# A cross-attention, self-attention and expert block: self-attention four slots later, batches normalised in two slots

## The chip, the core and the metric

One core of a Trainium2 chip. Its engines are TensorE (PE in the rows; PEld is its loading of weights), VectorE (DVE), ScalarE (ACT), GpSimd (POOL) and SyncE (SP), which issues most of the DMAs. Each runs its own list of instructions in order; semaphores tie the lists together. The metric is device time in microseconds; lower is better.

## What is computed

Eight batches of 64 latent rows of 512 attend to a context of 1601 rows, then to themselves, and then go through experts:

```python
def stablemax(x):
    s = jnp.where(x >= 0, x + 1.0, 1.0 / (1.0 - x))
    return s / jnp.sum(s, axis=-1, keepdims=True)
...
x = x + xattn(layernorm(x), ctx_1024, ...)   # 16 heads of 32, q, k, v, stablemax(q k / sqrt(32)) v, Wo
x = x + attn(layernorm(x), ...)              # 8 query heads of 64, one k and v, causal softmax, Wp
x = x + ffn(layernorm(x), ...)               # mean of 2 shared experts + top 2 of 8 routed, gelu, 512 -> 2048 -> 512
```

x is (8, 64, 512), ctx_1024 is (8, 1601, 512), all in float32.

## The kernel before

**Slots.** The first part is a list of 104 slots (`NCH`), 13 for each of 8 batches, one for each piece of 128 context rows and one for the tail of 65. I call a batch's slots r0 to r12; slot n is r(n mod 13) of batch n // 13. Every engine walks the same slots, `for n in range(NSLOT)`, with its own order of calls in a slot. Slots 104 to 135 hold the shared experts, and the routed experts come after them.

**Keys and values.** Context comes in 24 parts, three for a batch (r0 to r3, r4 to r7, r8 to r12). A part's keys and values are made from seven block products each (`product`, L928 and L931), Strassen's way. VectorE makes sums of the context (`context_sum`, L1572), ScalarE casts a block (`context_hi`, L1330), GpSimd subtracts the cast from it (`context_lo`, L685), TensorE multiplies, and VectorE joins the product into keys or values (`joined`, L1591 to L1611). In a part's first slot stand VectorE's three context sums for the next part, in its second the casts and subtractions of six blocks, in its third those of block 6. The key product for which a block is needed stands in the slots after.

**Scores and weights.** `scores` (L951) fills a bank for two pieces, in even slots of a batch; it waits until all earlier weights are made. ScalarE makes Relu, Ln and Exp of them (L1442, L1451, L1455), VectorE the weights (`weights`, L1623), TensorE the weighted values (`weighted`, L970), and GpSimd adds the weights up (`sums`, L731, in the slot after). The tail's scores are r12. After a batch, `denominators` (L981) and `normalised` (L1747 to L1761, five instructions for each half of the batch) finish it, three and four slots later.

**Self-attention.** Three of its four tiles (two batches each) run beside later batches. Their steps have fixed distances d from the first, `slot_of(t, d)`: the output projection and its stats (d=0, L996), the rows (d=1, L743 on GpSimd), their transposes (2, L1028), queries (3, L1037), keys and values (4), scores and masking (5), exponentials (5 and 6, on ScalarE), softmax and scaling (7, L1676 and L748), transposes (8), the attended values (9, L1077, then L1695 and L1697 on VectorE), the projection (11, L1091), the rows again (12), transposes (13) and gates (14). Before, tile t begins in slot 32 + 26 t, which is r6. `halved` says in which slots ScalarE casts the two output weights (L1368); GpSimd subtracts them one slot later (`output_weights_lo`, L758, the long one).

**Banks.** Products, and most steps of the self-attention, take one of three PSUM banks in turn (`pj`, `take`): each waits until VectorE has read what stood in its bank three uses ago.

**Experts.** A unit is a quarter of an expert's weights, 128x2048. It lands in a ring of eight; ScalarE casts it (`weights_hi`, L1378), VectorE subtracts (`weights_split`, L1721), and each copy has three places. `shared_up` (L1146), `gelu`, `hidden` (L1730, L1732) and `shared_down` (L1166) follow one another, two steps to a unit. The order in which VectorE takes the work of a slot is written out by hand:

```python
if n == NCH - 4:
    weights_split(0)
...
for p_ in products(n)[:before]:
    joined(*p_)
for m in group(n - 1)[1:] + group(n)[:1]:
    weights(m, 0)
    weights(m, 1)
for p_ in products(n)[before:]:
    joined(*p_)
...
for b, g, m in finished(n)[1]:
    normalised(b, g, m)
```

## Time and profile before

| | us |
|---|---|
| median of 3 runs (lowest, highest) | 1241.25 (1239.51, 1242.89) |
| the profiled execution | 1241.11 |
| its span, first to last instruction | 1239.4 |
| TensorE busy | 1210.2 (98%) |
| VectorE busy | 839.8 (68%) |
| ScalarE busy | 687.0 (55%) |
| GpSimd busy | 571.7 (46%) |

The busy shares are means over the whole span. In the stretch from 100 to 700 us GpSimd is busy some 70% and VectorE 74% of the time; in the stretch of the experts GpSimd hardly works. Idle time of an engine other than TensorE costs something only where TensorE waits for it, so the stops of TensorE are to be read one by one, with what the other engines did before each.

### The profile page before, as it was taken

The numbers are of one execution on the slowest core, as the hardware profiler recorded it, in microseconds if no ns is written. First come the engines' busy times: TensorE is split into PE (matmuls) and PEld (weight loads), VectorE is DVE, ScalarE is ACT, GpSimd is POOL, SyncE is SP. The second block draws the span as 40 slices with busy tenths as digits, with TensorE's granted clock in tenths as the row PEclk, the third lists the DMA queues.
The fourth block names the chain that finished last, engine by engine and source line by source line (L and its number), as shares of the span: only waits on it lengthen the run. The fifth ranks groups of instructions, "written<-read, shape, count | busy, mean of one in ns | idle before, by whom it ended". The sixth has DMA issues, their size and how long they took to land.

```text
span 1239.4 us, 33792 instructions
## 1 busy us (share of the span) xinstructions
PE 1210.2 (98%) x14478; PEld 1133.6 (91%) x14478; DVE 839.8 (68%) x1265; ACT 687.0 (55%) x1236; POOL 571.7 (46%) x357
## 2 busy tenths in 40 slices
PE   8999999999999999999999998999999999999998
PEld 7899999989999989999989997898889999999997
DVE  7666786776777686786785875766676455555655
ACT  4366656745755655756656557555644445544443
POOL 5656767776758776867766764000041001000000
PEclk9999999999999999999999998899999999999999
DMA  7331111121121212012112123745455599999991
GB/s 268 121 105 40 41 40 37 44 73 67 41 82 39 76 70 70 23 67 74 41 70 74 36 107 146 306 172 179 170 191 208 192 362 345 346 338 354 355 384 36
DMA packets 34794, 179.40 MB, mean 145 GB/s; under 512 B 6264, under 2 KB 9496, under 8 KB 15568
## 3 DMA queue, kind: packets, MB, share of 16 engines
q1 hardware_dynamic: 32896, 172.42, 38.0%
q0 software_dynamic: 1744, 4.76, 1.2%
q8 instruction: 117, 1.92, 0.6%
q14 instruction: 37, 0.30, 0.1%
HBM read 168.97 MB, written 8.19 MB: 143 GB/s over the span
## 4 chain that ended last, share of the span: by engine, by line
PE 91%; DVE 4%; issue 2%; POOL 1%; ACT 1%; DMA 0%; DVEq 0%; SPq 0%; POOLq 0%
PE bank L928 18%; PE bank L931 18%; PE bank L1285 12%; PE sc L1302 9%; PE sc L951 7%; PE sc L1146 7%; PE bank L970 4%; PE sc L1166 4%; PE bank L1166 4%; PE bank L909 1%; PE bank L1037 1%; DVE tt L1623 1%; POOL xn L731 1%; PE bank L1091 1%; PE bank L996 1%
## 5 line engine op out<-in xcount | busy, mean ns | idle before, releaser
L731 POOL TENSOR_TENSOR xn<-xn,tt 128x1024 f32<-128x1024 f32 x96 | 231.9, 2416 | 165.1 <-DVE tt L1623 163.3
L931 PE MATMUL bank<-wvh,blk 128*128 128x256 f32 x1344 | 248.8, 287 | 5.3 <-DVE va L1594 5.3
L928 PE MATMUL bank<-blk,wkh 128*128 128x256 f32 x1344 | 246.0, 285 | 0.0
L1721 DVE TENSOR_TENSOR wsl<-ring,wsh 128x2048 fp32r<-128x2048 f32 x72 | 165.2, 2294 | 112.6 <-ACT wsh L1378 109.8
L1442 ACT ACTIVATE tt<-sc 128x512 f32<-128x512 f32 (+1 forms) x208 | 107.8, 603 | 217.1 <-PE sc L951 209.3
L931 PEld LDWEIGHTS bank<-wvh,blk 128*128 128x128 f32 x1344 | 209.9, 192 | 8.8 <-DVE va L1594 6.1
L928 PEld LDWEIGHTS bank<-blk,wkh 128*128 128x128 f32 x1344 | 209.2, 192 | 4.2 <-issue 1.6
L931 PE MATMUL bank<-wvl,blk 128*128 128x256 f32 x672 | 190.6, 284 | 0.0
L928 PE MATMUL bank<-blk,wkl 128*128 128x256 f32 x672 | 190.0, 283 | 0.0
L1378 ACT CAST wsh<-ring 128x2048 fp32r<-128x2048 f32 x72 | 137.4, 1909 | 45.8 <-PE sc L1302 21.2
L1285 PEld LDWEIGHTS bank<-xT,ring 128*128 128x128 f32 x1280 | 144.8, 192 | 1.0
L1285 PE MATMUL bank<-xT,ring 128*128 128x128 f32 x1280 | 144.8, 275 | 0.0
L1623 DVE SCALAR_TENSOR_TENSOR tt<-sc,tt 128x512 f32<-128x512 f32 (+1 forms) x208 | 132.9, 680 | 0.8 <-ACT tt L1455 0.8
L931 PEld LDWEIGHTS bank<-wvl,blk 128*128 128x128 f32 x672 | 129.4, 193 | 0.0
L928 PEld LDWEIGHTS bank<-blk,wkl 128*128 128x128 f32 x672 | 128.8, 192 | 0.0
L685 POOL TENSOR_TENSOR blk<-bsum,blk 128x512 fp32r<-128x512 f32 x96 | 124.1, 1321 | 6.1 <-DVE bsum L1572 4.8
L1451 ACT ACTIVATE tt<-tt 128x512 f32<-128x512 f32 (+1 forms) x208 | 121.2, 644 | 0.0
L1455 ACT ACTIVATE tt<-tt 128x512 f32<-128x512 f32 (+1 forms) x208 | 120.9, 643 | 0.0
L951 PEld LDWEIGHTS sc<-qc,kk 32*128 32x128 f32 x3072 | 91.7, 189 | 11.9 <-DVE tt L1623 4.3
L951 PE MATMUL sc<-qc,kk 32*128 32x64 f32 x3072 | 98.3, 276 | 4.1 <-DVE tt L1623 4.1
L685 POOL TENSOR_TENSOR blk<-stg,blk 128x512 fp32r<-128x512 f32 x72 | 97.1, 1362 | 1.8 <-ACT blk L1330 1.8
L843 POOL DMA_INDIRECT yrows<-xT,tabi x7 | 6.9, 988 | 193.2 <-ACT xT L1518 193.2
(327 smaller groups left out, 2204.9 us busy)
## 6 DMA issues: line engine op xcount, KB each, us to landing
ring<-in_w SPq DMA_DIRECT2D x112, 1024.0 KB, 6.1
stg<-in_ctx SPq DMA_DIRECT2D x24, 1024.0 KB, 5.0
wqt<-in_wo SPq DMA_DIRECT2D x4, 1024.0 KB, 5.0
wqt<-in_aq SPq DMA_DIRECT2D x4, 1024.0 KB, 5.0
wqt<-in_ap_ SPq DMA_DIRECT2D x4, 1024.0 KB, 4.9
yrows<-K SPq DMA_DIRECT2D x1, 2048.0 KB, 12.4
bsum<-in_tails SPq DMA_DIRECT2D x2, 520.0 KB, 6.6
ktail<-bsum SPq DMA_DIRECT2D x1, 1040.0 KB, 4.1
```

The costliest lines, as they stand in the source:

```text
L685: e.tensor_tensor(block_lo(i, j), block_raw(i, j), block_hi(i, j).bitcast(F32), ALU.subtract).then_inc(s["cl_pool"], 1)
L731: e.tensor_tensor(dacc[0:kn, y, :], dacc[0:kn, y, :], tt[0:kn, w, :], ALU.add).then_inc(s["da_pool"], 1)
L928: m = e.matmul(dst[:, 256 * a:256 * a + 256], w[:, WPOS[j], c, r], x[:, c, :], start=(k_ == 0), stop=(k_ == 5))
L931: m = e.matmul(dst[:, 256 * a:256 * a + 256], x[:, c, r], w[:, WPOS[j], c, :], start=(k_ == 0), stop=(k_ == 5))
L951: m = e.matmul(sc[0:kn, h, c0 + 64 * g:c0 + 64 * g + 64], key, qc[r, g, 64 * b:64 * b + 64], start=True, stop=True)
L1285: m = e.matmul(bank[q % 2][:, P * jj:P * jj + P], ring[slot(un)][:, 512 * c + P * jj:512 * c + P * jj + P], xg[:, y, c, :], start=(c == 0) ...
L1302: m = e.matmul(bank[2][:], h_[:, j, :], w_[r_ % 3][:, 512 * jj:512 * jj + 512], start=(j == 0 and x_ == 0), stop=(j == 15 and x_ == 2))
L1378: e.copy(wsh[m % 3][:], ring[slot(un)][:]).then_inc(s["wh_act"], 1)
L1451: e.activation(tt[0:kn, w, r], tt[0:kn, w, r], ACT.Ln, bias=1.0).then_inc(s["ln_act"], 1)
L1455: e.activation(tt[0:kn, w, r], tt[0:kn, w, r], ACT.Exp, scale=-1.0).then_inc(s["ex_act"], 1)
L1623: e.scalar_tensor_tensor(t_, score_read(n, kn, hb), 0.0, t_, ALU.max, ALU.add).then_inc(s["f_dve"], 1)
L1721: e.tensor_tensor(wsl[m % 3][:], ring[slot(unit_split(m))][:], wsh[m % 3][:].bitcast(F32), ALU.subtract).then_inc(s["wl_dve"], 1)
```

## The change

The self-attention of tiles 0 to 2 begins four slots later (slot 36 + 26 t, which is r10), and so do its loads of weights. Only the gates of tile 2 stay in slot 104. The casts of the output weights move to three slots ahead of the first step and to d=6 (slots 33 and 42 for tile 0, where they were 27 and 37). A batch is normalised half in r3 and half in r5. ScalarE's cast of block 6 in r10 stands behind the exponentials, where it stood between Relu and Ln. At the end of the 104 slots VectorE splits unit 0 behind its weights of slot 100; unit 2 is copied and subtracted by VectorE alone (`weights_second`, in slots 100 and 102, the copy in place of ScalarE's in slot 104); the weights of piece 101 are made in slot 102. TensorE makes `shared_up(1)` in slot 102 and `shared_up(2)` in slot 104, where it made them in slots 103 and 106. The ring of three banks begins with bank 7, and the first tail value products wait accordingly. In the diff a line of semaphore names is cut; `first_dve` is added to it.

```diff
--- before.py
+++ after.py
@@ -107,8 +107,8 @@
             den.append(b)
             if last:
                 nrm.append((b, 0, 4))
-        if lag == 4 and not last:
-            nrm += [(b, 0, 2), (b, 2, 2)]
+        if lag in (4, 6) and not last:
+            nrm.append((b, lag - 4, 2))
     return den, nrm
 
 
@@ -120,7 +120,7 @@
 
 def halved(slot, what):
 
-    return next((t for t in range(3) if slot == (slot_of(t, 0) - 5, slot_of(t, 5))[what]), None)
+    return next((t for t in range(3) if slot == (slot_of(t, 0) - 3, slot_of(t, 6))[what]), None)
 
 
 def slot_of(t, d):
@@ -129,7 +129,7 @@
         return NCH + 2 + LAST_TILE[d]
     if t == 2 and d == 14:
         return NCH
-    return 2 * PER * t + 2 * PER + 6 + (9 if d == 10 else d)
+    return 2 * PER * t + 2 * PER + 10 + (9 if d == 10 else d)
 
 
 def tile(slot, d):
@@ -363,13 +363,13 @@
...
-        bank_read = [st.enter_context(nc.semaphore(f"bank{i}_read")) for i in (0, 1, 7)]
+        bank_read = [st.enter_context(nc.semaphore(f"bank{i}_read")) for i in (7, 0, 1)]
@@ -378,7 +378,7 @@
         ring_in = [st.enter_context(nc.semaphore(f"ring{i}_in")) for i in range(NR)]
         b1_in = [st.enter_context(nc.semaphore(f"b1_{k}_in")) for k in range(NBLK)]
 
-        pj = [bank[0], bank[1], bank[7]]
+        pj = [bank[7], bank[0], bank[1]]
         uses = projections()
         use = {u: n for n, u in enumerate(uses)}
         pob = bank[6]
@@ -418,6 +418,13 @@
         def unit_split(m):
 
             return m if m < 32 else unit_routed(*divmod(m - 32, 4), 1)
+
+        def wait_split(e, m):
+
+            if m == 2:
+                e.wait_ge(s["first_dve"], 2)
+            else:
+                e.wait_ge(s["wl_dve"], m + (m < 2))
 
         def slot(n):
             return n % NR
@@ -584,14 +591,14 @@
 
                 m = n - NR
                 if m < 32:
-                    e.wait_ge(s["wl_dve"], m + 1)
+                    wait_split(e, m)
                 else:
                     k, r = divmod(m - 32, 8)
                     kind, q = divmod(r, 4)
                     if kind == 0:
                         e.wait_ge(s["ru_pe"], 4 * k + q + 1)
                     else:
-                        e.wait_ge(s["wl_dve"], 32 + 4 * k + q + 1)
+                        wait_split(e, 32 + 4 * k + q)
 
             e.wait_ge(s["s_pe"], NCH - 1)
             load_shared(5)
@@ -899,7 +906,7 @@
                 dst, kn = take("vt", j), (8 if j == 4 else P)
                 col = 260 * (j // 2) + P * (j % 2)
                 if j < 3:
-                    e.wait_ge(s["kt_dve"], (10, 12, 8)[j])
+                    e.wait_ge(s["kt_dve"], (8, 10, 12)[j])
                 if j == 4:
                     e.wait_ge(s["tl_dve"], 3)
                 for c in range(4):
@@ -1127,7 +1134,7 @@
                 p, r = divmod(s_, NSH)
                 un = unit_shared(s_, 0)
                 if s_ % 2 == 0:
-                    e.wait_ge(s["wl_dve"], un + 1)
+                    wait_split(e, un)
                 if s_ < 2:
                     take("up", s_)
                 elif s_ < 4:
@@ -1152,13 +1159,13 @@
                 p, r = divmod(s_, NSH)
                 un = unit_shared(s_, 1)
                 if s_ % 2 == 0:
-                    e.wait_ge(s["wl_dve"], un + 1)
+                    wait_split(e, un)
                 e.wait_ge(s["hd_dve"], 2 * s_ + 2)
                 if s_ == 0:
                     e.wait_ge(s["f_dve"], 2 * NCH)
                 elif s_ == NSH:
                     e.wait_ge(s["un_dve"], NB)
-                    e.wait_ge(bank_read[2], reads_up_to(last_use(2)))
+                    e.wait_ge(bank_read[0], reads_up_to(last_use(0)))
                 for i in range(2):
                     for t in range(2):
                         c0 = 256 * i + P * t
@@ -1171,7 +1178,7 @@
             def positions():
 
                 e.wait_ge(s["rt_dve"], RT_SEL8)
-                for b_ in range(2):
+                for b_ in range(1, 3):
                     e.wait_ge(bank_read[b_], reads_up_to(last_use(b_)))
                 for t in range(4):
                     for t_ in range(t + 1):
@@ -1226,11 +1233,9 @@
                 if tile(n, 9) is not None:
                     for b in range(2):
                         attended(tile(n, 9), b)
-                if n == NCH - 1:
-                    shared_up(1)
                 for m in group_before(n):
                     weighted(m)
-                if NCH + 1 < n < NCH + 2 * NSH:
+                if NCH + 2 < n < NCH + 2 * NSH:
                     shared_up(n - NCH)
                 if tile(n, 2) is not None:
                     turn_rows(tile(n, 2))
@@ -1242,6 +1247,9 @@
                     product(*made_)
                 if n == NCH - 2:
                     shared_up(0)
+                    shared_up(1)
+                if n == NCH:
+                    shared_up(2)
                 if n == PLACE:
                     positions()
                 if n == PLACE + 2:
@@ -1295,7 +1303,7 @@
                 for q in range(4):
                     r_ = 32 + 4 * k + q
                     e.wait_ge(s["rh_dve"], 2 * (4 * k + q) + 2)
-                    e.wait_ge(s["wl_dve"], r_ + 1)
+                    wait_split(e, r_)
                     for jj in range(4):
                         j = 4 * q + jj
                         for x_, (h_, w_) in enumerate(((hTh, wsh), (hTh, wsl), (hTl, wsh))):
@@ -1441,8 +1449,6 @@
                     for hb in range(2):
                         e.activation(weights_view(m, kn, hb), score_read(m, kn, hb), ACT.Relu,
                                      scale=-1.0).then_inc(s["t_act"], 1)
-                if d == 2 and last and i + 1 < NPART:
-                    context_hi(i + 1, 6)
                 for m in group(n):
                     w, kn = m % TR, tokens(m)
                     for hb in range(2):
@@ -1453,6 +1459,8 @@
                         r = slice(512 * hb, 512 * hb + 512)
                         e.wait_ge(s["ln_act"], 2 * m + hb + 1)
                         e.activation(tt[0:kn, w, r], tt[0:kn, w, r], ACT.Exp, scale=-1.0).then_inc(s["ex_act"], 1)
+                if d == 2 and last and i + 1 < NPART:
+                    context_hi(i + 1, 6)
                 if d == 1 and i + 1 < NPART:
                     for j in ORDER[:6]:
                         context_hi(i + 1, j)
@@ -1474,9 +1482,7 @@
                     weights_hi(1)
                 if NCH <= n < NCH + 2 * NSH:
                     gelu(n - NCH)
-                    if n == NCH:
-                        weights_hi(2)
-                    elif n - NCH + 2 < 32:
+                    if NCH < n < NCH + 30:
                         weights_hi(n - NCH + 2)
                 if tile(n, 5) == 3:
                     for half in range(2):
@@ -1717,9 +1723,21 @@
                 e.tensor_tensor(gates[:, t, :], pj_of("g", t)[:, 0:8], rbt[:], ALU.add).then_inc(read_of("g", t), 1)
 
             def weights_split(m):
-                e.wait_ge(s["wh_act"], m + 1)
+                e.wait_ge(s["wh_act"], m + (m < 2))
                 e.tensor_tensor(wsl[m % 3][:], ring[slot(unit_split(m))][:], wsh[m % 3][:].bitcast(F32),
                                 ALU.subtract).then_inc(s["wl_dve"], 1)
+
+            def weights_second(lo):
+
+                if lo:
+                    e.wait_ge(s["v_pe"], PROD * NPART)
+                    e.wait_ge(s["first_dve"], 1)
+                    m = e.tensor_tensor(wsl[2][:], ring[slot(2)][:], wsh[2][:].bitcast(F32), ALU.subtract)
+                else:
+                    e.wait_ge(ring_in[slot(2)], ring_value(2))
+                    e.wait_ge(s["v_pe"], PROD * NPART - 5)
+                    m = e.tensor_copy(wsh[2][:], ring[slot(2)][:])
+                m.then_inc(s["first_dve"], 1)
 
             def hidden(s_):
                 e.wait_ge(s["ge_act"], s_ + 1)
@@ -1926,8 +1944,6 @@
                 last = i % PER_BATCH == PER_BATCH - 1
                 if n % PER == 0 and 0 < n <= NCH:
                     batch_sums(n // PER - 1)
-                if n == NCH - 4:
-                    weights_split(0)
                 if n == NCH - 1:
                     weights_split(1)
                 if d == 0 and i + 1 < NPART:
@@ -1976,18 +1992,24 @@
                 before = ((2, 1, 2, 1, 1) if last else (2, 0, 2, 0))[d]
                 for p_ in products(n)[:before]:
                     joined(*p_)
+                if n == NCH - 2:
+                    weights_second(1)
+                    weights(n - 1, 0)
+                    weights(n - 1, 1)
                 for m in group(n - 1)[1:] + group(n)[:1]:
-                    weights(m, 0)
-                    weights(m, 1)
+                    if m != NCH - 3:
+                        weights(m, 0)
+                        weights(m, 1)
                 for p_ in products(n)[before:]:
                     joined(*p_)
                     if p_ == ("v", i, 4) and i + 1 < NPART:
                         context_sum(i + 1, 3)
+                if n == NCH - 4:
+                    weights_split(0)
+                    weights_second(0)
                 for b, g, m in finished(n)[1]:
                     normalised(b, g, m)
 
-                if n == NCH + 1:
-                    weights_split(2)
                 if NCH <= n < NCH + 2 * NSH:
                     hidden(n - NCH)
                     if n > NCH and n - NCH + 2 < 32:
```

## Rows read from the trace of the kernel before

**Rows 1.** The page, busy time, share of the span and instructions of each engine.

```profile
PE 1210.2 (98%) x14478; PEld 1133.6 (91%) x14478; DVE 839.8 (68%) x1265; ACT 687.0 (55%) x1236; POOL 571.7 (46%) x357
```

**Rows 2.** TensorE's own waits: line, releaser, us in total, times, longest us.

```profile
PE sc L951 <- DVE tt L1623: 10.2, 8, 4.1
PE bank L931 <- DVE va L1594: 5.3, 3, 1.8
PE bank L909 <- issue: 2.6, 1, 2.6
...
PE bank L981 <- POOL xn L731: 1.3, 1, 1.3
...
PE sc L1166 <- issue: 0.8, 1, 0.8
```

**Rows 3.** Windows: us, each engine's busy us (instructions), TensorE's clock, DMA share, GB/s.

```profile
262.30:265.60 3.30, 3.30 (x17) 3.30 (x17) 3.20 (x7) 1.02 (x2) 1.93 (x1) 0.50 0.03 7
...
753.80:760.60 6.80, 5.32 (x128) 5.20 (x128) 2.03 (x4) 1.48 (x4) 2.36 (x1) 0.50 0.09 17
```

**Rows 4.** A window with L928 alone: us, TensorE matmul and weight load, clock, DMA.

```profile
242.00:253.00 11.00, 10.34 (x84) 10.13 (x84) 1.00 0.32 110
```

**Rows 5.** A window with L996 alone, the same columns.

```profile
268.00:273.00 5.00, 2.97 (x12) 2.19 (x12) 1.00 0.05 8
```

**Rows 6.** Timeline of VectorE, slot 29: start us, us, engine, line, operation, tiles, count.

```profile
253.08 0.94 DVE L1747 RECIPROCAL xT<-xT 128x128 f32<-128x128 f32 x1
254.06 2.00 DVE L1751 TENSOR_TENSOR xT<-xT 128x128 f32<-128x128 f32 x1
...
258.78 0.29 DVE L1761 TENSOR_TENSOR cTl<-xT,cTh 128x128 fp32r<-128x128 f32 x1
```

**Rows 7.** Timeline of TensorE: scores of r8, r10, tail (bare batch), tail (attention beside it).

```profile
196.99 2.01 PE L951 MATMUL sc<-qc,kk 32*128 32x64 f32 x64
...
208.78 2.01 PE L951 MATMUL sc<-qc,kk 32*128 32x64 f32 x64
...
219.74 0.70 PE L951 MATMUL sc<-qc,ktb 32*65 32x64 f32 x32 [0.54 <-DVE tt L1623]
...
315.32 0.70 PE L951 MATMUL sc<-qc,ktb 32*65 32x64 f32 x32 [1.32 <-DVE tt L1623]
```

**Rows 8.** Timeline of ScalarE, r10 of the bare batch.

```profile
210.94 2.07 ACT L1442 ACTIVATE tt<-sc 128x512 f32<-128x512 f32 x4 [0.98 <-PE sc L951]
213.54 0.62 ACT L1330 CAST blk<-stg 128x512 fp32r<-128x512 f32 x1 [0.53 <-PE bank L931]
...
217.20 1.13 ACT L1455 ACTIVATE tt<-tt 128x512 f32<-128x512 f32 x2
```

**Rows 9.** Timeline of GpSimd: two sums, a block subtraction, the weights' subtraction, a scaling.

```profile
193.73 4.91 POOL L731 TENSOR_TENSOR xn<-xn,tt 128x1024 f32<-128x1024 f32 x2
...
217.77 1.31 POOL L685 TENSOR_TENSOR blk<-stg,blk 128x512 fp32r<-128x512 f32 x1
...
246.43 4.63 POOL L758 TENSOR_TENSOR wol<-wqt,woh 128x2048 fp32r<-128x2048 f32 x1
...
326.68 1.05 POOL L748 TENSOR_TENSOR sm<-sm,rs 128x512 f32<-128x512 f32 x1 [4.37 <-DVE rs L1676]
```

**Rows 10.** Timeline of VectorE: a context sum and a cast beside GpSimd, a sum alone.

```profile
43.86 1.77 DVE L1572 TENSOR_TENSOR bsum<-stg 128x512 f32<-128x512 f32 x1
...
46.46 1.23 DVE L1826 CAST blank<-xa 128x15 f32<-128x15 int32 x1
...
198.78 0.69 DVE L1572 TENSOR_TENSOR bsum<-stg 128x512 f32<-128x512 f32 x1 [1.00 <-DMA stg<-in_ctx]
```

**Rows 11.** Timeline of VectorE, slot 100.

```profile
750.97 2.46 DVE L1721 TENSOR_TENSOR wsl<-ring,wsh 128x2048 fp32r<-128x2048 f32 x1 [1.57 <-ACT wsh L1378]
```

**Rows 12.** Timeline of GpSimd and VectorE, slot 44.

```profile
362.47 2.08 POOL L743 TENSOR_SCALAR xa<-xres,mv,rstd 128x512 f32<-128x512 f32 x1
...
363.20 0.68 DVE L1572 TENSOR_TENSOR bsum<-stg,bsum 128x512 f32<-128x512 f32 x1
```

More of the change, by code:

```diff
@@ L365, in build @@
             "exp_act woh_act xh_act gap_act wT_act ge_act wh_act rg_act yh_act "
-            "eps_dve iota_dve ones_dve cs_dve un_dve wkl_dve wvl_dve tl_dve kt_dve bias_dve xr_dve f_dve "
+            "eps_dve iota_dve ones_dve cs_dve un_dve first_dve wkl_dve wvl_dve tl_dve kt_dve bias_dve xr_dve f_dve "
             "cr_dve bn_dve xn_dve xa_dve xt_dve sm_dve oh_dve nrm_dve xl_dve rt_dve hd_dve "
```

## The prediction

> **What bounds the kernel now.** I read the page first: TensorE is busy 98% of the span [rows 1], so the end moves only if its stops, its clock or its work change. The change leaves TensorE's work as it is. The list of TensorE's own waits comes next [rows 2]: 10.2 us before the scores (L951), 5.3 us before value products (L931), 2.6 us at the start (L909), 1.3 and 0.8 us at the hand-over to the experts. With smaller ones that is about 24 us in a span of 1239.4; from 777 us to 1231 us there is no stop over 0.1 us, so all that can be won or lost lies in the first 777 us, and a microsecond of stop there is a microsecond of the end. Third, the granted clock: after some stops it falls from 2.4 to 1.2 GHz for 3.4 or 6.8 us [rows 3]; every microsecond of work in such a stretch loses half a microsecond. It did so after the stop before L909 and after the 4.1 us stop, after one of three stops of 1.75 us and one of five of 1.3 us.
>
> I write r0 to r12 for the slots of a batch. A product lasts 1.48 us (7 in 10.34) [rows 4], the output projection 2.9 us [rows 5].
>
> **What it saves.**
> (a) Batches normalised in two slots. Vector's ten instructions of the batch before, at the end of r3, last 6.0 us (253.08 to 259.07) in the slots 29, 55 and 81, since the first tensor_tensor takes 2.00 us instead of 0.29 while GpSimd runs [rows 6]; the copy of value product 0 comes late and product 3 waits for its bank: 5.3 us in 3 stops [rows 2]. Half the work, 2.1 us, now goes to r5, and GpSimd's 4.63 us subtraction [rows 9] no longer stands in r2, so the first half is free of it too. The copy ends before it is wanted: -5.3 us, and the half clock after the first of these stops [rows 3] goes with it, -1.7 us.
> (b) The stop before the tail's scores (r12) is 1.32 us with the self-attention's masking beside it and 0.54 us in a bare batch [rows 7]. All become bare: 3 x 0.78, -2.3 us. The 0.54 stays: it is the joining of a key product and then the weights, on Vector, not ScalarE's cast, which is also moved.
> (c) The end. Vector's split of unit 0 (2.46 us, after 1.57 us of waiting for ScalarE) stands ahead of the weights for which the scores wait 4.1 us [rows 11, 2]. Placed behind them, the stop becomes the 0.6 us of (b). Unit 2 split early lets its first product fill the stretch before the denominators. But shared_up(1) no longer covers ScalarE's and Vector's 4.8 us from the tail's scores to its weights: 2.6 us of small matmuls are left, so 2.2 to 2.4 us of stop. Then 1 us each before the down product 0 and the output of tile 3 and about 1 us before the down product 2 (Vector's halving waits for the table loads after the root). Stops and half clock of before there are 6.4 and 5.6 us; what I get for after is 7.0 us. I take -5 us; bounds -8 and 0.
> (d) Ring turned: the first tail value product waits for kt_dve 8, not 10, and starts when TensorE is free, but the transposes behind still wait for kt_dve 16. Between 0 and -1.4 us: -0.7.
> Together -15.0 us.
>
> **What it costs.**
> (e) Rows for the self-attention, now r10 to r12. TensorE reaches r10 at S (208.78 in a bare batch, [rows 7]), spends 2.9 us on the output, and starts its scores at S+2.9. ScalarE begins 2.16 us later; Relu, Ln and Exp of both tiles last 6.2 us without the cast between them [rows 8], to S+11.3. The cast of block 6 (0.62 us), which stood between Relu and Ln, now comes only here: S+11.8. GpSimd, in its own order, must then subtract block 6 (1.31 us) [rows 9], add a sum (2.4 us), and only then make the rows (a TENSOR_SCALAR, 2.08 us) [rows 12]: S+17.6. TensorE has done tail scores and two weighted tiles at S+15.5 (219.74 - 208.78 + 2.9 + 1.66) and stands at the transposes, three key products queued behind: 2.1 us of stop, three times, +6.3. Lower bound 0.5 us each if the cast's place didn't matter, upper 3.
> (f) Second half of the normalising, r5, before the attention's output in r6. Vector's instruction with two SBUF inputs, or a CAST, ends only when GpSimd's running tensor_tensor ends: the last of three sums beside GpSimd took 1.77 us instead of 0.69, a 15-element CAST 1.23 us [rows 10]. In r5 GpSimd runs its six block subtractions without a pause, 1.3 us each, and it is late there: scaling (1.05 us) waits for Vector and holds up a sum, then the 4.63 us subtraction [rows 9]. With P the start of r4's scores, GpSimd starts the train at P+15.7; Vector starts its half at P+15.4, passes the reciprocal (0.94 us, not held: [rows 6]) and then pays one GpSimd instruction for each of four: done at P+21.0 instead of P+17.5, and two of its four copies of the attended rows (0.43 us each) free the first bank at P+21.9. TensorE wants it for the second key product at P+18.7. That is 3.2 us for tiles 0 and 1, and 0.8 us for tile 2, whose batch has two instructions fewer: +7.2, bounds 2 and 11.
> (g) GpSimd's other 4.63 us subtraction moves from r2 to r8. It starts when two sums end (198.64) [rows 9], and Vector's first context sum is issued at 198.78 [rows 10]. The sum is held to 203.3, the third ends at 205.1, value product 0 is joined at 205.8; TensorE wants its bank at 204.4 (scores at 196.99 [rows 7], plus 3.0, plus three products). 1.4 us in three batches: +4.2, bounds 0 and 6.
> (h) In the four batches without attention in r6 the half of (f) delays the joining of key product 0, which the fourth needs. Vector frees it at about P+21.9, TensorE wants it at P+20.7; one GpSimd boundary earlier there is no stop. Half of 4 x 1.2: +2.4, bounds 0 and 5.
> (i) Clock. Two stops over 3 us, three of 2.1 and one of 2.4: by the shares above some three falls, 1.7 us each, less what the followers catch up: +4, bounds 0 and 9.
> Moved at no cost: ScalarE's two casts of output weights (1.9 us, in r3 and r7, where it idles 7 us), the three loads of weights on SyncE (each has two slots to land in; the context loads behind them wait for GpSimd anyway; in the last batch they now follow the experts' first three loads, by which they are not delayed), the joins, which keep their order.
>
> A row where a page and the trace part: Vector's sum beside GpSimd's TENSOR_SCALAR (L743) took 0.68 us, not held at all [rows 12]. The Trainium skill (SBUF — State Buffer, two separate sides) says that the shared port pair is an exclusive lock for the whole instruction, against any GpSimd instruction that reads SBUF. By the page the split of unit 0 in slot 100, which meets L743, would wait about 1 us more and the end would gain 4 us rather than 5; by the row it doesn't, and the sum above goes by the row.
>
> **Sum.** -15.0 + 6.3 + 7.2 + 4.2 + 2.4 + 4 = +9.1 us on the profiled execution's 1241.11 (span 1239.4 and 1.7 around it): 1250.2. The median shown is 1241.25, so I say 1250.
>
> **Rivals.**
> (1) The holding of Vector doesn't reach TensorE (it decides at P+18.7: if Vector has freed the attended bank by then, and the context sums of r8 slip in before GpSimd's long subtraction). Then (f), (g), (h) are nothing and (i) about 2: 1241.1 - 15 + 6.3 + 2 = 1234.4; with (g) alone left, 1239. For it: GpSimd and Vector meet only within tenths. Against: GpSimd has no idle time in r5 in any batch. Faster, 0.25, mostly 1233 to 1237.
> (2) Savings and costs cancel: two of (e) to (h) at their lower bounds, or one halved and the clock never falling: 1238 to 1244. 0.17.
> (3) The hand-over is worse: up(0) waits for the bank of the third transposes, which Vector reads only behind two 2.3 us instructions, and the saving of (c) is 0; with the clock falling often: 1256 to 1262. 0.10.
> (4) All stops go as the placing suggests and no new ones come: 1241.1 - 19 (with the 4.1 us stop's full 9 us): 1222 to 1230. 0.05.
> The forecast itself, 1245 to 1256, has 0.43. Range 1233 to 1258.
>
> About 0.3% (3.7 us) can be told from no change. Faster by more: rival 1 without its upper tail and rival 4, 0.26. Within: rival 2 and that tail, 0.21. Slower: the forecast and rival 3, 0.53.
>
> **What would show it.** Gone: the stops before L931 in r4, the 1.32 us ones, the 4.1 us one. New, in the list of TensorE's waits: three of about 2 us before the transposes of self-attention rows (L1028 of before) put down to GpSimd's rows; two of 3 us before a key product (L928), released by Vector's L1697; three of 1.4 us before L931 in r8. In Vector's rows: the tensor_tensors of the second half at 1.2 us instead of 0.29, and a context sum of over 4 us in r8. It is wrong if those rows are short, or if GpSimd has its rows ready when TensorE comes.

## The result, and the profile after

| | before | after |
|---|---|---|
| median, us (lowest, highest) | 1241.08 (1239.51, 1242.89) | 1253.95 (1253.73, 1256.09) |
| ratio, with its 95% interval | | 1.0108 (1.0092 to 1.0124) |
| the profiled execution, us | 1241.11 | 1256.09 |
| its span, us | 1239.4 | 1254.3 |

The changed kernel is 1.1% slower; 1250 was forecast. The profiled execution of after is the slowest of its four, so what follows explains 14.9 us of span, of which the medians show 12.9.

First TensorE's own waits after the change (line, releaser, us in total, times, longest us). Lines have moved by some seven: L935 and L938 are the key and value products, L958 the scores, L977 the weighted values, L1014 transposes at the start, L1035 the transposes of self-attention rows, L1173 the experts' down product.

```profile
PE bank L1035 <- POOL xa L750: 6.2, 3, 2.1
PE bank L935 <- DVE oTl L1703: 5.9, 2, 2.9
PE sc L958 <- DVE tt L1629: 5.0, 9, 0.6
PE bank L935 <- DVE kk L1597: 4.6, 4, 1.1
PE sc L1014 <- DVE bsum L1554: 2.8, 1, 2.8
PE bank L977 <- DVE tt L1629: 2.2, 1, 2.2
PE bank L938 <- DVE va L1600: 2.0, 3, 0.8
...
PE sc L1173 <- DVE hl L1750: 1.4, 1, 1.4
```

Beside [rows 2] the reader sees what left: of 10.2 us before the scores 5.0 remain, the three stops before the value product in r4 are gone, and those of the hand-over shrank from 6.4 to 5.4 us, the scores' there included. What came is larger: the first, second, fourth and seventh row, 18.7 us. All stops together (over 0.1 us, without the 1.1 us ahead of TensorE's first instruction) are 34.9 us; they were 23.8.

The granted clock, in the windows in which it fell after such a stop (columns as in [rows 3]):

```profile
312.30:315.70 3.40, 3.40 (x19) 3.40 (x17) 1.21 (x2) 0.00 (x0) 1.79 (x1) 0.51 0.02 5
373.80:377.20 3.40, 3.40 (x19) 3.40 (x18) 2.50 (x6) 0.00 (x0) 3.40 (x3) 0.50 0.00 0
561.50:564.90 3.40, 3.40 (x18) 3.40 (x17) 2.49 (x6) 0.00 (x0) 3.40 (x3) 0.50 0.02 5
786.80:793.60 6.80, 6.58 (x60) 6.22 (x64) 3.89 (x5) 5.72 (x7) 4.63 (x3) 0.50 0.35 113
```

The first follows one of the three 2.1 us stops, the second and third the two of 2.9 us, the last the 2.2 us stop of the hand-over. Each 3.4 us at 1.2 GHz, with TensorE busy throughout, costs 1.7 us.

Where the second kind of stop comes from stands in the timelines of slot 43 (r4) to 45 (r6), first VectorE's (start us, us, engine, line, operation, tiles, shapes, count, idle before it and its releaser):

```profile
366.72 0.94 DVE L1765 RECIPROCAL xT<-xT 128x128 f32<-128x128 f32 x1
367.70 0.72 DVE L1769 TENSOR_TENSOR xT<-xT 128x128 f32<-128x128 f32 x1
368.46 1.27 DVE L1775 TENSOR_TENSOR xT<-xT,bvt 128x128 f32<-128x128 f32 x1
369.76 1.19 DVE L1777 CAST cTh<-xT 128x128 fp32r<-128x128 f32 x1
370.98 1.26 DVE L1779 TENSOR_TENSOR cTl<-xT,cTh 128x128 fp32r<-128x128 f32 x1
372.17 0.41 DVE L1701 CAST oTh<-bank 128x256 fp32r<-128x256 f32 x1
372.61 0.42 DVE L1703 TENSOR_TENSOR oTl<-bank,oTh 128x256 fp32r<-128x256 f32 x1
```

then GpSimd's and TensorE's in the same stretch:

```profile
366.99 2.59 POOL L692 TENSOR_TENSOR blk<-stg,blk 128x512 fp32r<-128x512 f32 x2
369.53 5.09 POOL L692 TENSOR_TENSOR blk<-bsum,blk 128x512 fp32r<-128x512 f32 x4
...
373.09 0.50 PE L935 MATMUL bank<-blk,wkh 128*128 128x256 f32 x2 [2.94 <-DVE oTl L1703]
```

Where nothing holds them the tensor_tensors last 0.29 us [rows 6] and the cast 0.23 us, as this row of the kernel before shows:

```profile
256.42 0.23 DVE L1759 CAST cTh<-xT 128x128 fp32r<-128x128 f32 x1
```

Here the four last 0.72, 1.27, 1.19 and 1.26 us: each ends with the block subtraction of GpSimd (1.3 us) beside it, the first having come in the middle of one. The two instructions behind them (L1701, L1703) read the PSUM bank and take 0.41 and 0.42 us in the midst of GpSimd's next subtractions, not held. The attended values wait behind the four, and TensorE waits for their bank. That is step (f), as forecast.

The context sum of r8 beside GpSimd's long subtraction, VectorE and then GpSimd:

```profile
282.94 4.87 DVE L1578 TENSOR_TENSOR bsum<-stg 128x512 f32<-128x512 f32 x1
287.85 0.69 DVE L1578 TENSOR_TENSOR bsum<-stg,bsum 128x512 f32<-128x512 f32 x1
...
282.66 4.61 POOL L765 TENSOR_TENSOR wol<-wqt,woh 128x2048 fp32r<-128x2048 f32 x1
```

The sum, alone 0.69 us [rows 10], ends 0.54 us after GpSimd does. Of this kind of holding the Trainium skill (SBUF — State Buffer, SBUF: two separate sides) says that whichever of the two starts first has the shared ports for its whole instruction, where VectorE's has two SBUF inputs or runs in a two-port mode. By that rule, the trace agrees for the rows above in how the wait ends (with an instruction of GpSimd, never shared out). The first sum's row names stg once since both of its inputs lie there.

### The profile page after: what moved, and what is told of

It is laid out like the page before. It is cut to its first block, busy times and chain, and to the rows that moved or that the text cites. A ratio compares the mean times of both kernels' runs of the same rounds, so it can differ in the third digit from the quotient of the medians.

```text
span 1254.3 us, 33794 instructions
## 1 busy us (share of the span) xinstructions
PE 1214.3 (97%) x14478; PEld 1135.4 (91%) x14478; DVE 873.1 (70%) x1266; ACT 685.0 (55%) x1235; POOL 574.0 (46%) x357
## 4 chain that ended last, share of the span: by engine, by line
PE 77%; DVE 10%; issue 6%; POOL 5%; DMA 1%; ACT 1%; SPq 0%; DVEq 0%; POOLq 0%; ACTq 0%
PE bank L938 14%; PE bank L935 14%; PE bank L1293 11%; PE sc L1310 9%; PE sc L1153 7%; PE sc L958 5%; PE bank L1173 4%; PE sc L1173 3%; PE bank L977 3%; POOL blk L692 2%; POOL xn L738 2%; DVE tt L1629 1%; DVE bsum L1578 1%; PE bank L1044 1%; PE bank L916 1%
## 5 line engine op out<-in xcount | busy, mean ns | idle before, releaser
L935 PE MATMUL bank<-blk,wkh 128*128 128x256 f32 x1344 | 251.0, 288 | 10.6 <-DVE oTl L1703 5.9
L938 PE MATMUL bank<-wvh,blk 128*128 128x256 f32 x1344 | 247.8, 286 | 2.1 <-DVE va L1600 2.0
L935 PEld LDWEIGHTS bank<-blk,wkh 128*128 128x128 f32 x1344 | 212.7, 195 | 16.4 <-DVE oTl L1703 6.3
L938 PEld LDWEIGHTS bank<-wvh,blk 128*128 128x128 f32 x1344 | 208.8, 191 | 5.9 <-DVE va L1600 2.7
L935 PE MATMUL bank<-blk,wkl 128*128 128x256 f32 x672 | 192.1, 286 | 0.0
L938 PE MATMUL bank<-wvl,blk 128*128 128x256 f32 x672 | 190.0, 283 | 0.0
L935 PEld LDWEIGHTS bank<-blk,wkl 128*128 128x128 f32 x672 | 130.9, 195 | 0.0
L938 PEld LDWEIGHTS bank<-wvl,blk 128*128 128x128 f32 x672 | 128.7, 192 | 0.0
L958 PEld LDWEIGHTS sc<-qc,kk 32*128 32x128 f32 x3072 | 90.1, 187 | 8.3 <-issue 2.2
L958 PE MATMUL sc<-qc,kk 32*128 32x64 f32 x3072 | 96.7, 273 | 0.5 <-DVE tt L1629 0.5
```

Source lines behind the costliest of these rows:

```text
L935: m = e.matmul(dst[:, 256 * a:256 * a + 256], w[:, WPOS[j], c, r], x[:, c, :], start=(k_ == 0), stop=(k_ == 5))
L938: m = e.matmul(dst[:, 256 * a:256 * a + 256], x[:, c, r], w[:, WPOS[j], c, :], start=(k_ == 0), stop=(k_ == 5))
L958: m = e.matmul(sc[0:kn, h, c0 + 64 * g:c0 + 64 * g + 64], key, qc[r, g, 64 * b:64 * b + 64], start=True, stop=True)
```

## The experiments

Two theories. **Mine:** VectorE's instructions on SBUF are held by whatever GpSimd runs beside them, and GpSimd's rows come late, so each new stop belongs to one named pair of instructions and goes with it. **The rival:** VectorE or GpSimd has simply too much work in these slots, and a stop that is removed comes back one slot later. Each run was timed beside the kernel before; ratios are to that.

### ScalarE's cast of block 6 where it was

```diff
+                if d == 2 and last and i + 1 < NPART:
+                    context_hi(i + 1, 6)
                 for m in group(n):
                     w, kn = m % TR, tokens(m)
...
-                if d == 2 and last and i + 1 < NPART:
-                    context_hi(i + 1, 6)
```

> The changed kernel with ScalarE's cast of block 6 in r10 back between Relu and Ln; nothing else. Theory (GpSimd's order behind a late cast): the three stops of 2.1 us before the self-attention's transposes shrink to about 0.5 us, since GpSimd has block 6 by S+9 and then waits only for the weights; 1254.0 becomes 1248 to 1250, with one clock fall fewer. Rival (GpSimd has simply too much work in r9 to r11, wherever the cast stands): the stops stay at 2 us and the time at 1254.

1246.35 us (1242.50 to 1250.26), ratio 1.0047 (1.0031 to 1.0062). TensorE's waits of this kernel:

```profile
PE bank L935 <- DVE oTl L1703: 5.9, 2, 3.0
...
PE bank L935 <- DVE kk L1597: 4.6, 4, 1.2
...
PE bank L1035 <- POOL xa L750: 1.6, 3, 0.5
```

The three stops of 2.1 us are now 0.5 us, and no other stop changed by more than 0.5 us but one of 1.0 us at the hand-over, which is new: the cast's place made 4.7 us of stops. The median fell by 7.6 us, more than that, since the clock falls less often: in the profiled run it fell once after the start, for 3.4 us.

### GpSimd's rows ahead of its sums

```diff
+                if tile(n, 1) is not None and tile(n, 1) < 3:
+                    rows(1, tile(n, 1))
                 if 1 <= n < NCH + 1:
                     sums(n - 1)
...
-                if tile(n, 1) is not None and tile(n, 1) < 3:
-                    rows(1, tile(n, 1))
```

> The changed kernel with GpSimd making the self-attention's rows ahead of the sum in the same slot (r11) instead of behind it. Theory: rows end at S+15.3 instead of S+17.6 and TensorE comes at S+15.5: the three stops of 2.1 us go, 1254.0 becomes 1246 to 1248. Rival (ScalarE's root or the stats are late, not GpSimd's order): the stops stay. Rival 2 (the postponed sum is wanted sooner): a new stop of up to 2 us elsewhere in r12 or r0.

1246.41 us (1244.14 to 1249.36), ratio 1.0045 (1.0030 to 1.0060). The wait for GpSimd's rows is gone from the list altogether (6.2 us), and no new one of over 0.3 us appeared. So the order in GpSimd's queue, cast then subtraction then sum then rows, is the whole of step (e). This run has less stop than the last (29.1 us for 29.9) and the same time: its clock fell three times after the start, for 17 us together.

### All of the batch normalised in r3 again

```diff
-        if lag in (4, 6) and not last:
-            nrm.append((b, lag - 4, 2))
+        if lag == 4 and not last:
+            nrm += [(b, 0, 2), (b, 2, 2)]
```

> The changed kernel with a batch normalised in one slot again (r3), self-attention still four slots later. Theory (the half in r5 is held up by GpSimd's block subtractions): both stops of 2.9 us in r6 and the four of 1.14 us go, with two clock falls; in r4 at most 0.2 us comes back, since GpSimd's long subtraction no longer makes its sums late in r3: 1239 to 1242. Rival (the stop in r6 comes from the two banks that the attended rows take, whatever Vector did before): the 2.9 us stay, and the three 1.75 us stops in r4 return: 1254 to 1260.

1252.93 us (1249.52 to 1253.80), ratio 1.0089 (1.0071 to 1.0106): the time was missed by 11 us. Its waits:

```profile
PE bank L1035 <- POOL xa L750: 6.3, 3, 2.1
...
PE bank L935 <- POOL blk L692: 4.1, 7, 0.7
...
PE bank L938 <- DVE va L1600: 2.8, 3, 1.3
```

Both stops for the attended values' bank and all four before the joining of the first key product went (10.5 us), so the half in r5 made steps (f) and (h). But two others grew behind them: GpSimd's block subtractions now come late before the key products of r6, and the value product in r8 waits 1.3 us instead of 0.8 in two of three batches, as TensorE arrives without the stop ahead (in the third 0.2 us, behind a new wait of 0.7 us before L977). Stops fell only from 34.9 to 31.1 us. The three 1.75 us stops of r4 did not come back although all ten instructions stand in r3 again: in the kernel before they were not the ten instructions' doing alone. My mechanism held, and the rival holds for over half of the gain.

### GpSimd's first long subtraction in r2 again

```diff
-    return next((t for t in range(3) if slot == (slot_of(t, 0) - 3, slot_of(t, 6))[what]), None)
+    return next((t for t in range(3) if slot == (slot_of(t, 0) - 9, slot_of(t, 6))[what]), None)
```

> The changed kernel with the first cast of output weights and GpSimd's 4.6 us subtraction in the slots where they were before (27 and 28 for tile 0, r1 and r2), not in r7 and r8. Theory (Vector's context sum in r8 is held by that subtraction): the stops of 0.5 to 0.8 us before L938 in r8 go, -2 us, 1252; the first half of the normalising is held by 1.7 us again but no stop follows from it. Rival (the r8 stops are a consequence of the later r5 half alone): they stay, 1254.

1260.45 us (1256.40 to 1261.04), ratio 1.0146 (1.0127 to 1.0164), slower than the changed kernel by 6.5 us where 2 us less were expected. The stops in r8 went, as my theory said, but one wait grew:

```profile
PE bank L935 <- DVE kk L1597: 7.9, 4, 2.3
```

It was 4.6 us; three of its four stops are now 2.2 us. In sum the stops are 36.0 us, 1.1 more than in the changed kernel. What made it slower is the clock: it fell nine times in the profiled run, five times in the changed kernel's. So this 4.6 us instruction costs stops in both slots in which it stood. That isn't so in every slot: behind the one for the second output weight, where the kernel before has it (here tile 0's), no stop came for 84 us.

```profile
317.69 4.62 POOL L758 TENSOR_TENSOR wol<-wqt,woh 128x2048 fp32r<-128x2048 f32 x1
```


### The end alone, on the kernel before

The kernel before with the hunks of the diff that touch the experts' first units and the weights of slots 101 and 102. The ring of banks stays as it was; the text below names it among the edits, but the run left it out.

```diff
+                if n == NCH - 2:
+                    weights_second(1)
+                    weights(n - 1, 0)
+                    weights(n - 1, 1)
...
+                if n == NCH - 4:
+                    weights_split(0)
+                    weights_second(0)
...
                     shared_up(0)
+                    shared_up(1)
+                if n == NCH:
+                    shared_up(2)
```

> The kernel before with the edits of the end alone (splits of units 0 to 2, order of the weights of slots 101 and 102, shared_up(1) and (2) earlier, ring of banks turned); self-attention, casts and normalising as before. Theory: the end's saving doesn't depend on the rest: the 4.1 us stop becomes about 0.6, a stop of about 2.3 us comes between shared_up(2) and the weighted values, three of about 1 us at the experts; 1241 less 2 to 5 us, 1236 to 1239, less if the half clock after 787 us stays as long as 6.8 us. Rival (the end's saving is given back in the experts whatever stands ahead): 1241, no change.

1236.49 us (1233.61 to 1238.26), ratio 0.9966 (0.9956 to 0.9976), on a kernel before of 1240.42: 3.9 us faster. The waits and the clock at the hand-over:

```profile
PE bank L977 <- DVE tt L1629: 2.2, 1, 2.2
...
PE sc L1173 <- DVE hl L1750: 1.4, 1, 1.4
```

```profile
770.23:773.64 3.41, 3.41 (x17) 3.20 (x16) 3.31 (x2) 3.39 (x5) 2.88 (x2) 0.50 0.24 41
```

Step (c) is right in mechanism and size: the 4.1 us stop is 0.5 us, and 2.2 us come behind `shared_up(2)`. The routed experts begin 4.3 us earlier relative to the first batch. In the changed kernel the same stop was followed by 6.8 us of half clock instead of 3.4, and 1.7 us of this gain were lost.

### Two slots of normalising alone, on the kernel before

The diff is the third experiment's, turned round.

> The kernel before with the batches normalised in two slots (r3 and r5) and nothing else. The self-attention of before begins in r6, so no attended values wait for a bank in r6; GpSimd's subtraction of the first output weight still stands in r2. Theory: the three stops of 1.75 us before the value product in r4 go (-5.3 us); the half in r5 meets GpSimd's train of block subtractions, is held, and the joining of the first key product of r6 comes 1 us late in each of the seven batches: +7 to +8 us of stops of 1.1 us. 1241 -5.3 +7.5 and one or two more half-clock stretches: 1243 to 1247. Rival (the holding is no cost without the attention beside it): 1241 -5.3 = 1236, and no stop over 0.5 us before the key products of r6.

1269.16 us (1268.01 to 1269.64), ratio 1.0230 (1.0213 to 1.0247). Both numbers given were far off. TensorE's waits and, below, VectorE in slot 31 (r5):

```profile
PE bank L996 <- issue: 26.4, 3, 8.8
```

```profile
268.24 0.94 DVE L1747 RECIPROCAL xT<-xT 128x128 f32<-128x128 f32 x1
...
271.36 1.17 DVE L1759 CAST cTh<-xT 128x128 fp32r<-128x128 f32 x1
272.56 2.33 DVE L1761 TENSOR_TENSOR cTl<-xT,cTh 128x128 fp32r<-128x128 f32 x1
```

I had overlooked who reads the second half: the self-attention's output projection, the first step of r6 in the kernel before. TensorE stands at it for 8.8 us in each of three batches; the clock fell 2.2 to 2.4 us into each of these stops and stayed low for 10.2 us, 3.6 to 3.8 of them with TensorE back at work; the last of the held instructions waits for a sum of GpSimd, 2.33 us. The stops of r4 did go. So the two edits belong together: normalising in two slots is possible only with the self-attention later.

### The self-attention four slots later alone, on the kernel before

```diff
-    return 2 * PER * t + 2 * PER + 6 + (9 if d == 10 else d)
+    return 2 * PER * t + 2 * PER + 10 + (9 if d == 10 else d)
...
-    return next((t for t in range(3) if slot == (slot_of(t, 0) - 5, slot_of(t, 5))[what]), None)
+    return next((t for t in range(3) if slot == (slot_of(t, 0) - 3, slot_of(t, 6))[what]), None)
```

> The kernel before with the self-attention (and its loads and casts) four slots later, and nothing else: all of a batch still normalised in r3, ScalarE's cast of block 6 where it was, the end as before. Theory: the three stops of 1.32 us before the tail's scores become 0.54 (-2.3 us); the rows of r11 come late by GpSimd's sum alone, 0.5 us (three times) since the cast is early; GpSimd's 4.63 us subtraction, now in r8, holds a context sum: three stops of 1.3 us before value products in r8 and, behind it, about 0.65 us twice a batch in r6 (three batches) as in the run with one slot of normalising. The 1.75 us stops of r4 are not there, because they came of the subtraction in r2. 1241 -2.3 -5.3 +1.5 +4 +4 = 1243, and up to three more half-clock stretches: 1243 to 1249. Rival (the 1.75 us stops come of the ten instructions standing in one slot, whatever GpSimd does): they stay, and the time is 1248 to 1254.

1248.16 us (1246.15 to 1250.49), ratio 1.0056 (1.0039 to 1.0073), inside what was expected, and the stops that were named are there (in r8 two of three at their size, the middle one 0.4 us):

```profile
PE sc L951 <- DVE tt L1623: 8.1, 8, 4.3
PE bank L928 <- POOL blk L685: 4.0, 6, 0.7
PE bank L931 <- DVE va L1594: 3.0, 3, 1.3
...
PE bank L1028 <- POOL xa L743: 1.6, 3, 0.5
```

The 1.75 us stops before L931 in r4 went with GpSimd's subtraction out of r2, with all ten instructions still in one slot; the rival is out for these. But the sum of stops doesn't give the time. They are 27.4 us against 23.8 before, the clock was low for as long (but before, 1.5 us of it lay in a stop and cost nothing), and the span is 9.4 us longer. The larger part is in no stop: from the tail of the second batch to that of the fourth TensorE took 177.2 us outside its stops and half clock before, and 179.2 us here, with as many instructions. Over the three tiles that is 5.2 us (2.0, 2.1 and 1.1). By pairs of neighbouring matmuls it lies in front of products and of L1077, in steps of 0.1 to 0.25 us, and behind each listed stop the next matmul starts some 0.15 to 0.27 us late. I call these small waits; which of them has which cause I can't tell from the trace. They don't come with the later self-attention alone. Counted in the same way against "the end alone" (the kernel before in the first two stretches), they are 3.0 us in the changed kernel, 5.3 us with all of a batch normalised in r3 again, and 0.9 us with the first long subtraction back in r2, though the self-attention is late in all three. So the place of that subtraction bears on them as well; how much stays open, since the last of these kernels also had 24 us of half clock in these stretches, where such waits could hide, and the changed one 10 us.

### The second half in r6

```diff
-        if lag in (4, 6) and not last:
-            nrm.append((b, lag - 4, 2))
+        if lag in (4, 7) and not last:
+            nrm.append((b, 2 * (lag > 4), 2))
```

> The changed kernel with the second half of the normalising one slot later, in r6, where GpSimd's train of block subtractions has ended. Theory: the held half was the cause of the two 2.9 us stops (attended values' bank) and of four 1.1 us ones before the key products of r6; with the half out of r5 they go: -10.5 us of stops and one clock stretch less, but the value products' stops in r8 grow from 0.7 to 1.3 us (three times, +1.5): 1254 -10.5 -1.7 +1.5 = 1243, range 1241 to 1247. Rival (Vector is late there for the amount of its work in r4 to r6, not for the holding): the stops move by a slot and the time stays at 1252 to 1256.

1263.77 us (1261.12 to 1265.76), ratio 1.0186 (1.0168 to 1.0204). My number was 20 us too low and even the rival's too low. The stops of steps (f) and (h) went and larger ones came: 9.2 us before the attended values' projection (3 times) and 3.7 us before scores (4 times). VectorE in r6, and GpSimd:

```profile
377.01 1.20 DVE L1769 TENSOR_TENSOR xT<-xT 128x128 f32<-128x128 f32 x1
378.24 2.35 DVE L1775 TENSOR_TENSOR xT<-xT,bvt 128x128 f32<-128x128 f32 x1
...
378.02 2.42 POOL L738 TENSOR_TENSOR xn<-xn,tt 128x1024 f32<-128x1024 f32 x1
```

The train of block subtractions has ended there, but GpSimd's sums stand in its place, and each holds an instruction for 2.4 us. I had priced the slot by its block subtractions alone.

### The long subtraction in halves, with the end's edits

The experiments say: the end is a gain by itself, the rest is not, and GpSimd's 4.6 us instruction makes stops as long as it is whole. So: the kernel of "the end alone", and

```diff
+                for h in range(2):
+                    c = slice(2 * h, 2 * h + 2)
+                    if part is None or part == h:
+                        e.tensor_tensor(wol[:, c, :], wqt[:, c, :], woh[:, c, :].bitcast(F32),
+                                        ALU.subtract).then_inc(s["wol_pool"], 1)
...
+                for part in range(2):
+                    for t in range(3):
+                        if n == slot_of(t, 0) - (6, 4)[part]:
+                            output_weights_lo(t, 0, part)
```

> The kernel before with the edits of the end alone, as in b1_end_only, and one more: ScalarE's cast of the first output weight in r12 of the batch before, and GpSimd's 4.63 us subtraction of it in two halves of 2.3 us, one in r0 and one in r2, where all of it stood in r2. Theory: the stops of 1.78 us before the value product in r4 come of GpSimd: its sum of 2.37 us runs beside Vector's first tensor_tensor of the normalising because the 4.63 us stood ahead of it; 2.3 us earlier it ends before Vector comes. The three stops go (-5.3 us) and the half clock after the first (-1.7 us), and in r0 a context sum of Vector's is held by at most 2.3 us, which the 1.4 us it has in hand and the next slot take up to a stop of 0 to 0.5 us. 1236.5 - 7 + 0 to 1.5: 1229.5 to 1231. Rival (the ten instructions in one slot are the cause, not GpSimd): the three stops stay, 1236 to 1238.

1228.86 us (1227.95 to 1229.67), ratio 0.9898 (0.9882 to 0.9915): 1.0% faster than the kernel before, and by the medians 2.0% faster than the changed one. GpSimd's two halves and the sums behind the second, then VectorE's context sum in r0 and its start of the normalising in slot 29 (r3):

```profile
227.04 2.38 POOL L768 TENSOR_TENSOR wol<-wqt,woh 128x1024 fp32r<-128x1024 f32 x1
...
246.51 2.41 POOL L768 TENSOR_TENSOR wol<-wqt,woh 128x1024 fp32r<-128x1024 f32 x1
248.87 4.93 POOL L738 TENSOR_TENSOR xn<-xn,tt 128x1024 f32<-128x1024 f32 x2
...
228.52 1.45 DVE L1585 TENSOR_TENSOR bsum<-stg 128x512 f32<-128x512 f32 x1
...
253.66 0.29 DVE L1776 TENSOR_TENSOR xT<-xT 128x128 f32<-128x128 f32 x1
```

In [rows 6] that tensor_tensor took 2.00 us. The sum now ends as VectorE comes, the three stops are gone and with them the half clock, and the price is one context sum of 1.45 us in r0, which no one waits for. The stops are 17.6 us. The rival is out for these three stops. What isn't shown is that the halving did it and not the place: the first half also stands in r0 now, and the whole instruction in r0 was never run.

### The changed kernel with all of it

One slot of normalising, rows ahead of sums, first subtraction in halves in r0 and r2, second in halves in r4 and r6.

```diff
+                        if n == slot_of(t, 0) - (10, 8)[part]:
+                            output_weights_lo(t, 0, part)
...
+                        if n == slot_of(t, 0) + (7, 9)[part]:
+                            output_weights_lo(t, 1, part)
```

> The changed kernel with the batch normalised in one slot again, the rows of r11 ahead of GpSimd's sums, and both long subtractions in halves: the first in r0 and r2 of the batch of r10, the second in r4 and r6 behind it (whole in r8 and r4 in the changed kernel). Theory: what remained in the run with one slot of normalising were stops that GpSimd's two 4.6 us instructions and the late rows made (1.3 x 2 + 0.7, 1.3 x 3, 2.1 x 3, 0.9): they go, stops fall from 30.2 us to some 18, and with them two of four half-clock stretches: 1253 - 12.5 - 3.4 = 1237, and since the kernel with the end alone has 22.1 us of stops at 1236.5, down to 1232. I say 1231 to 1238. Rival (GpSimd's work must stand somewhere, and each place holds Vector in turn): stops of 0.5 to 1.5 us in r1, r3, r5 or r7, and 1240 to 1248.

1233.89 us (1232.12 to 1236.12), ratio 0.9937 (0.9920 to 0.9953). The long stops are gone here too and 18.6 us are left, yet the version with the later self-attention is still 5.0 us behind the one that leaves it in r6 (6.4 us by the spans of the profiled executions). Of the 6.4, 1.7 us is half clock (6.8 us at the hand-over for 3.4) and 1.0 us is stop; the other 3.7 us lie outside both, as the small waits did (1.4, 1.3 and 1.0 us in the three stretches).

## Why the prediction was right, and where its terms were not

The ledger, on the profiled executions (span +14.9):

| step | forecast | measured |
|---|---|---|
| (a) stops of r4, and the half clock after the first | -7.0 | -7.0 |
| (b) tails | -2.3 | -2.3 |
| (c) end | -5 | -4.3 alone; -2.6 with the longer half clock of the changed kernel |
| (d) ring | -0.7 | 0 |
| (e) rows late | +6.3 | +6.2 |
| (f) attended values' bank | +7.2 | +6.0 |
| (g) long subtraction in r8 | +4.2 | +2.0 |
| (h) joining in the other batches | +2.4 | +4.6 |
| (i) clock | +4 | +5.1 |
| small waits | none | +2.9, the remainder (+3.0 counted in the stretches above) |
| sum | +9.1 | +14.9 |

**Right in mechanism and size:** (a), (b) and (e), to a tenth of a microsecond, and (f) for tiles 0 and 1 (2.9 us for 3.2). The experiments show (e) by itself twice; (f) and (h) went together with the half in r5. Of (a) the cause is now told more sharply: halving the work of r3 wasn't needed, since taking GpSimd's 4.6 us from in front of the sum removed the same stops.

**(f), third tile:** 0.8 was said, 0.15 measured.

**(g)** was costed as if TensorE came to r8 on time. It comes 1.1 us late from the stops of (h), which take their share first: 0.79, 0.47 and 0.79 us instead of 1.4. Where the stops of (h) were taken away, those of (g) grew to 1.3 us in two of three batches, near the size I had given them. Terms (g) and (h) are one chain and not two summands.

**(h)** was entered at half, because one GpSimd boundary decided it. All four happened, 1.14 us each. The coin did not fall four times: the order of the engines' work is the same in each of these batches, and VectorE's last instruction waited there for a sum of 2.4 us, not for a subtraction of 1.3:

```profile
188.89 2.40 POOL L738 TENSOR_TENSOR xn<-xn,tt 128x1024 f32<-128x1024 f32 x1
...
189.04 2.40 DVE L1779 TENSOR_TENSOR cTl<-xT,cTh 128x128 fp32r<-128x128 f32 x1
```

An all-or-nothing term that repeats with the batches should have been entered whole, as 0 or 4.8.

**(d)** was wrong. The stop at the start moved from L909 (2.6 us) to L1014, the transposes behind (2.8 us). This edit was never run alone.

**(i)** The forecast of three falls was right (one after a 2.1 us stop, two after 2.9 us), 1.7 us each; the reduction for followers that catch up was wrong, as none did. The same 2.2 us stop at the hand-over was followed by 3.4 us at 1.2 GHz in one kernel and 6.8 us in another, which moved (c).

**Not in the sum:** the small waits. The prediction opened by saying that the change leaves TensorE's work as it is, and that only stops and clock count. The instructions are the same, but the self-attention alone, moved, took 5.2 us more of TensorE's time outside any stop, and the whole change some 3 us. It is the largest thing I did not see, and its cause is only located, not settled.

**How near by luck.** The sum's 1250.2 lies 5.9 us under the profiled execution and 3.8 us under the median. It would have been further off had (g) and (h) not missed by 2.2 us each in opposite directions. The terms of the clock are partly chance, too: the half clock in all was equally long before and after (20.5 us each), since what (i) added, (a) and (c) took away.

**The row against the rule.** For the split of unit 0 the prediction went by a row in which a TENSOR_SCALAR of GpSimd did not hold VectorE, against the rule that it cites. The changed kernel has that very pair:

```profile
768.29 2.09 POOL L750 TENSOR_SCALAR xa<-xres,mv,rstd 128x512 f32<-128x512 f32 x1
...
769.22 2.28 DVE L1727 TENSOR_TENSOR wsl<-ring,wsh 128x2048 fp32r<-128x2048 f32 x1
```

VectorE's 2.28 us are what this instruction takes among the experts, where GpSimd hardly works (2.29 us). It was not held, and the row was right.

Rival (1), that the holding would not reach TensorE, failed at the point it named: VectorE freed the bank at 373.0, TensorE wanted it at 370.2. Rival (3) has its mark in the half clock of 6.8 us alone; `shared_up(0)` waited 0.3 us. Rivals (2) and (4) needed the stops of (e) to (h) small or absent; they were 18.8 us where 20.1 were forecast. The sign stands on (e) to (h): without these four kinds of stop and their clock the changed schedule would be at or below the kernel before, as the last experiment shows.

## What to carry to other kernels

Two engines whose instructions hold each other, as VectorE's and GpSimd's do here, should be read as pairs: before moving VectorE's SBUF work, look at what GpSimd runs in the new slot, sums too, and before moving a long GpSimd instruction, try cutting it, for the harm of an instruction of 4.6 us was undone by two of 2.4 us in different slots (-0.6% with one small edit). Test the parts of a composite change singly and also ask which depend on each other: here the end alone gained 0.3% and the split alone lost 2.3%, because another part supplied the slack it needs. When a schedule's stops add up and its span does not, compare the bottleneck engine's time outside its stops, stretch by stretch.

## What the runs showed of the hardware that was not expected

A GpSimd instruction holds a context sum of VectorE for all of its 4.6 us, and the sum ends 0.54 us behind it (0.55 us behind a 2.38 us one), so the held instruction seems to do nearly all its 0.69 us of work after the release.

The clock makes most of the spread between executions of one kernel. The version with the cast put back ranged over 7.8 us in 8 runs with stops of 0.5 to 3 us, at a mean granted clock of 0.998 of full speed in the fastest and 0.992 in the slowest; the version with no stop over 1.4 us between the start and the hand-over ranged over 1.7 us in 4. And the number of falls isn't told by the sum of the stops: with nearly equal sums one kernel's clock fell five times and another's nine. After stops of 2.1 us it fell once in three in the changed kernel, twice in three in the one with the long subtraction in r2. A stop is therefore worth its length, the late restart behind it, and by chance 1.7 or 3.4 us more.
